# The triangular inverse of a gated delta-rule layer: T accumulated in its bank with one gathered weight tile per couple of batches, and the lists of a step reordered on four engines

## The reference

```
S = S * exp(g_t)                 # decay per key channel
err = k_t . S
S = S + k_t (x) beta_t (v_t - err)
o_t = q_t . S
```

## Time and profile before

| what | value |
|---|---|
| median of 3 runs | 5741.74 us (5737.70 to 5747.36) |
| the profiled execution | 5738.22 us, its span 5736.4 us |
| TensorE busy | 5429.4 us, 95% |
| VectorE busy | 4294.1 us, 75% |
| ScalarE busy | 3051.8 us, 53% |
| GpSimd busy | 1782.9 us, 31% |

### The profile page before, as it was taken

The page is one execution under the profiler, slowest core; times in us unless marked ns, Lnnn a source line. Parts: engine busy times, 40 slices in busy tenths (PEclk is TensorE's granted clock), DMA queues, the critical chain, the costliest instruction groups (busy, mean ns, idle before and its releaser), DMA issues. The chain is left out here.

```text
span 5736.4 us, 86704 instructions
## 1 busy us (share of the span) xinstructions
PE 5429.4 (95%) x28996; PEld 3752.5 (65%) x28996; DVE 4294.1 (75%) x8413; ACT 3051.8 (53%) x5964; POOL 1782.9 (31%) x1767
## 2 busy tenths in 40 slices
PE   5599999999999999999999999999999999799999
PEld 2377777777777777777777777777777777344444
DVE  7688888888888888888888888888888888121110
ACT  3466666666666666666666666666666665100110
POOL 2233333333333333333333333333333333000000
PEclk8799999999999999999999999999999999899999
DMA  2101111111111111111111111111111110331221
GB/s 77 47 29 38 30 38 30 38 30 36 30 36 30 35 30 38 30 38 30 38 30 38 30 37 31 32 37 30 38 30 38 30 30 19 107 112 52 72 75 50
DMA packets 192034, 235.65 MB, mean 41 GB/s; under 512 B 41577, under 2 KB 136425, under 8 KB 187505
## 3 DMA queue, kind: packets, MB, share of 16 engines
q1 hardware_dynamic: 111016, 188.22, 10.9%
q10 hardware_dynamic: 80584, 41.95, 2.5%
HBM read 183.75 MB, written 46.38 MB: 40 GB/s over the span
## 5 line engine op out<-in xcount | busy, mean ns | idle before, releaser
L720 PE MATMUL bank<-xT,weights 128*128 128x512 f32 x4096 | 2126.0, 606 | 33.2 <-PEq L155 33.2
L1465 POOL TENSOR_TENSOR KR<-KR,decay_u 128x256 f32<-128x256 f32 x768 | 691.2, 900 | 1536.4 <-PE bank L739 1536.4
L739 PEld LDWEIGHTS bank<-KQ,KR 128*128 128x128 f32 x7168 | 914.7, 191 | 266.0 <-issue 241.8
L739 PE MATMUL bank<-KQ,KR 128*128 128x128 f32 x7168 | 961.1, 276 | 16.3 <-DVE KQ L1040 15.4
L1040 DVE TENSOR_TENSOR KQ<-KQ,decay_u 128x512 f32<-128x512 f32 x896 | 746.2, 833 | 291.9 <-PE bank L739 291.0
L1025 DVE SCALAR_TENSOR_TENSOR conv<-pre,taps,conv 128x512 f32<-128x512 f32 x1152 | 936.8, 813 | 18.0 <-ACT conv L1254 8.3
L1055 DVE COPY_PREDICATED all_pairs<-level_mask,bank 128x512 f32<-128x512 int32 x896 | 792.8, 885 | 0.0
L720 PEld LDWEIGHTS bank<-xT,weights 128*128 128x128 f32 x4096 | 663.0, 192 | 185.9 <-issue 164.2
L762 PEld LDWEIGHTS bank<-T_inv,pairs 128*128 128x128 f32 x1536 | 270.9, 190 | 563.2 <-ACT T_inv L1319 323.0
L762 PE MATMUL bank<-T_inv,pairs 128*128 128x128 f32 x1536 | 495.2, 407 | 109.6 <-ACT T_inv L1319 109.4
L1319 ACT ACTIVATE T_inv<-bank 128x256 fp32r<-128x256 f32 x640 | 247.5, 387 | 454.0 <-PE bank L780 451.9
(11 more groups left out here) (190 smaller groups left out, 8963.4 us busy)
## 6 DMA issues: line engine op xcount, KB each, us to landing
decay_u<-decay_scratch SPq DMA_DIRECT2D x128, 510.0 KB
beta_u<-beta_scratch SPq DMA_DIRECT2D x128, 256.0 KB
y_in<-y_scratch SPq DMA_DIRECT2D x32, 1024.0 KB, 4.8
y_scratch<-y_rn ACTq DMA_DIRECT2D x112, 256.0 KB, 2.3
xt<-in_L_attn_hidden_states SPq DMA_DIRECT2D x8, 1024.0 KB, 5.3
x_in<-in_L_attn_hidden_states SPq DMA_DIRECT2D x28, 256.0 KB, 5.0
out<-o_out ACTq DMA_DIRECT2D x28, 256.0 KB, 2.0
w<-in_L_ffn_W SPq DMA_DIRECT2D x8, 704.0 KB, 4.8
```

Source lines behind the costliest of these rows:

```text
L720: last = nc.tensor.matmul(bank[w % 2][:], weights[par][:, w, k, :], xT[:, k, u % J * UC:(u % J + 1) * UC], start=k == 0, stop=k == KC - 1)
L739: last = nc.tensor.matmul(to[:, :, i], KR[:, cols(i)], halves(KQ[:, :, cols(i)], l, 1), start=True, stop=True)
L1465: nc.gpsimd.tensor_tensor(firsts, firsts, second.to_broadcast([P, 2, UC >> (l + 2), 1 << l]), ALU.mult).then_inc(keys_scaled.sem, 1)
```

## The change

X is kept in another order: its tile now has the turned batches first (2, 3, 0, 1; in_x), and so have the first pairs. T is no longer computed afresh from X. Bank 5 keeps T over the levels and each level adds to it. For this the product's weights are XX, a tile of 256 columns: for each couple the second sides of the natural batch's X and the first sides of the turned one's, side by side, gathered by three GpSimd copies (gather_x). The moving operand is Z without the identity, copied from its bank by ScalarE (keep_z). Z now lies in the upper half of bank 2. The first T comes from X by two matmuls of 256 columns, with a permutation that swaps neighbours as weights and neighbouring columns swapped in the moving operand (first_t); ScalarE takes it, and VectorE's first_inverse is gone. T and X of a level are separate entries of TensorE's list, and all four lists are reordered. ZI waits for keep_z, except at level 6.

```diff
@@ setup (GpSimd)
-            nc.gpsimd.tensor_copy(ident_r[:], ident[:])
+            nc.gpsimd.tensor_copy(swap_r[:].rearrange("p (m two) -> p m two", two=2)[:, :, ::-1],
+                                  ident[:].rearrange("p (m two) -> p m two", two=2))
@@ TensorE
-                for i in range(B):
-                    last = nc.tensor.matmul(bank[5][:, cols(i)], pairs_first[:, cols(i)], ident_r[:], start=True, stop=True)
+                for turned in range(2):
+                    to = slice(turned * (UC // 2), (turned + 1) * (UC // 2))
+                    at = in_x(turned * COUPLES) * P
+                    swapped = X[m % 2][:, at:at + UC // 2].rearrange("p (n two) -> p n two", two=2)[:, :, ::-1]
+                    last = nc.tensor.matmul(bank[5][:, to], swap_r[:], swapped, start=turned == 0, stop=turned == 1,
+                                            skip_group_check=True)
...
+            def inverse_t(l):
+                wait(pe, z_kept, b, l)
+                wait(pe, xx_ready, b, l)
+                for r in range(COUPLES):
+                    last = nc.tensor.matmul(firsts_in_place(bank[5], l, r), XX[:, cols(r)], Z[:, cols(r)],
+                                            start=False, stop=True, skip_group_check=True)
+                last.then_inc(t_done.sem, 1)
...
-                if l < LEVELS - 1:
-                    for i in range(B):
-                        last = nc.tensor.matmul(bank[5][:, half_cols(i)], X[b % 2][:, cols(i)],
-                                                halves(ZI[:, cols(couple(i))], l, i // COUPLES), start=True, stop=True)
-                    last.then_inc(t_done.sem, 1)
@@ VectorE
-                nc.vector.tensor_tensor(T_inv[:], bank[5][:], ident_each[:], ALU.add).then_inc(t1_ready.sem, 1)
...
-                wait(dve, z_done, b, l)
+                if l < LEVELS - 1:
+                    wait(dve, z_kept, b, l)
+                else:
+                    wait(dve, z_done, b, l)
@@ ScalarE
+            def keep_z(l):
+                wait(act, z_done, b, l)
+                nc.scalar.activation(Z[:], bank[2][:, UC // 2:UC], ACT.Copy).then_inc(z_kept.sem, 1)
...
+                nc.scalar.activation(all_first_sides(T_inv, l + 1), all_first_sides(bank[5], l + 1),
+                                     ACT.Copy).then_inc(t_ready.sem, 1)
@@ GpSimd
+        def gather_x(u, l, before):
+            if l >= 2:
+                wait_apart(pool, x_ready.sem, x_ready.at(u, l - 1), pool_waits_passed)
+                wait_apart(pool, t_done.sem, t_done.at(u, l), pool_waits_passed)
...
+            natural, turned = X[u % 2][:, UC // 2:], X[u % 2][:, 0:UC // 2]
+            nc.gpsimd.tensor_copy(halves(XX[:], l, 1), halves(natural, l, 1).bitcast(F32))
+            for i in range(COUPLES, B):
+                last = nc.gpsimd.tensor_copy(halves(XX[:, cols(couple(i))], l, 0),
+                                             halves(X[u % 2][:, cols(in_x(i))], l, 0).bitcast(F32))
+            last.then_inc(xx_ready.sem, 1)
```

More of the change, by code:

```diff
@@ L805, in apply_inverse @@
                 for i in range(B):
-                    last = nc.tensor.matmul(bank[7][:, cols(i)], X[u % 2][:, cols(i)], to[:, cols(i)], start=True, stop=True)
+                    last = nc.tensor.matmul(bank[7][:, cols(i)], X[u % 2][:, cols(in_x(i))], to[:, cols(i)], start=True, stop=True)
                 return last
@@ L918, in step @@
             level(0)
-            inverse_xt(1)
+            inverse_t(1)
             refine(c, 1)
+            inverse_x(1)
             project(2, (3,))
@@ L963, in step @@
             project(1, (2,))
[L964 removed]
+            first_t()
             project(1, (3,))
@@ L1395, in store_output @@
                                   by_batch(y_out[:])[:, :, 0:1], allow_slow_non_contiguous=True).then_inc(y_stored, 16)
+            keep_z(1)
             silu_v()
-            take_t(1)
+            take_t(b, 1)
             take_x(1)
+            keep_z(2)
+            take_projection(2)
+            take_t(b, 2)
+            take_x(2)
             store_output()
-            take_projection(2)
+            keep_z(3)
+            take_t(b, 3)
+            take_x(3)
+            keep_z(4)
             first_tap(2)
[L1403 to L1406, removed]
             silu_squares(0)
@@ L1409, in step @@
                 tail_squares()
+            take_x(4)
+            take_t(b, 4)
             square_output()
+            keep_z(5)
             silu_gate()
-            take_t(4)
-            take_x(4)
             silu_squares(1)
-            take_t(5)
+            take_t(b, 5)
             take_x(5)
@@ L1430, in step @@
             keep_all_pairs()
+            take_t(m, 0)
             take_projection(1)
@@ L1489, in step @@
                 squares_left(s.a, 1)
+                for l in range(2, LEVELS - 1):
+                    gather_x(s.b, l, None)
                 return
[L1491 to L1496, removed]
+            scale_keys(s.m, 1 - s.odd, 0)
+            gather_x(s.b, 2, None)
+            scale_keys(s.m, 1 - s.odd, 1)
+            gather_x(s.b, 3, None)
+            scale_keys(s.m, 1 - s.odd, 2)
+            gather_x(s.b, 4, None)
+            scale_keys(s.m, 1 - s.odd, 3)
+            first_x(s.m, s.c)
+            gather_x(s.b, 5, None)
+            scale_keys(s.m, 1 - s.odd, 4)
+            squares_left(s.a, 0)
+            scale_keys(s.m, 1 - s.odd, 5)
+            squares_left(s.a, 1)
+            scale_keys(s.m, 1 - s.odd, 6)
+            gather_x(s.m, 1, s.b)
         walk(pool, step)
```

163 lines of the change are left out of this document (92 added, 71 removed).

## The result

The changed kernel takes 5584.61 us (median of 4 runs, 5584.41 to 5589.27) where the kernel before takes 5743.07 beside it: ratio 0.9726, 95% interval 0.9710 to 0.9743. That is 158 us gained; 5540 was forecast, some 200 us. The direction and the range held; one term of the sum, the new waits, was off by half a microsecond a step.

What follows compares the result with a forecast made beforehand. TensorE was taken as the bound, VectorE close behind. Per step, 1.20 us less work and 0.37 less idle (0.97 old, 0.60 new) make 1.57, over 128 steps 201 us: 5540 us, own range 5495 to 5590, overall range 5450 to 5660.

Steps and rivals of the forecast that it cites:

- the new waits: TensorE's new small waits on ScalarE's copies, GpSimd's gathers and VectorE, put at 0.60 us a step.
- T's matmuls: TensorE, levels 1 to 5: twenty matmuls of 64 columns become ten of 128, removing 1.05 us a step.
- First T: TensorE: four matmuls of 128 columns become two of 256, between 0.11 us lost and 0.22 gained; 0.15 gained was taken.
- The split of T from X: Two visits of TensorE add no matmul; five more changes of kind cost 0 to 0.25 us, taken as 0.0.
- The old wait: TensorE's idle before Z, 0.82 us a step, ended by ScalarE's T copy; at Z(5) it goes as the silu moves.
- ScalarE's chain Z, copy, T: From Z's start through ScalarE's copy to T: 0.92 us, fitting TensorE's 1.08 us with 0.15 to spare.
- 0.8 hides with 0.3 to spare: GpSimd's gather of 0.8 us between X of one level and T of the next makes TensorE wait for nothing.
- Point 6: VectorE: 31.7 us of work in a step of about 34.6, late once or twice around levels 4 and 5.
- Rival 2: VectorE takes over as gathers hold it up: step 35 to 35.7 us, time 5600 to 5685; chance 0.20.
- rival 3: Slower: gathers on GpSimd delay T(2) to T(5); 1.9 us each gives 5870, 2.4 us gives 6130; chance 0.07.
- Rival 4: No effect: a wait at the step's end, from chain sums to level 0, sets the period; 5740; chance 0.03.
- Rival 1: Waits go wholly and TensorE's work shrinks by the upper bounds: at most 293 us, 5449; chance 0.14.

Runs made afterwards that it cites:

- experiment 4: The changed kernel with each T matmul of 128 columns issued as two of 64, same result: 5714.23 us, ratio 0.9952.
- Experiment 5: The kernel before with only ScalarE's square_output() and silu_gate() moved behind take_t(4) and take_x(4): 5650.77 us, ratio 0.9836.
- experiment 3: The changed kernel with each GpSimd gather cut to one copy of 2 columns, so T is computed from wrong weights: 5563.23 us, ratio 0.9685.
- experiment 1: The changed kernel with take_delta() put ahead of take_projection(0) in ScalarE's list: 5501.08 us, ratio 0.9583.
- experiment 2: The changed kernel with VectorE's tap convolve(1, (1,)) moved from ahead of ZI(4) to behind keep_pairs(3): 5631.18 us, ratio 0.9805.
- experiment 7: The changed kernel with take_delta() ahead of take_projection(0) and VectorE's gated_output() behind the two taps: 5464.24 us, ratio 0.9509.

## Why the prediction was right or wrong

- T's matmuls: 1.05 was taken, 0.95 measured by start to start (5 x 0.19), 1.01 by experiment 4. Right.
- First T: 0.15 taken, 0.16 measured (0.80 to 0.64). Right in the difference, by luck in part: the two prices that it came from were 0.44 and 0.22 to 0.55, and both groups take more from start to start. They start about 0.45 into the projection ahead, which takes 0.90 before a level; with it they take 1.25 and 1.10.
- The split of T from X costs nothing that can be seen: T's pairs take 0.25, X's 0.22 to 0.30 and 0.41 behind a projection at level 6, Z's 0.26 to 0.61 depending on what stands ahead, as before.
- The old wait: it went, as said, through the gate's place. It was worth more than its idle column, which is what the sum took. Experiment 5 gained 0.75 a step from it, of which 0.49 was idle time. That explains why busy time fell by 1.42 when 1.20 of work was forecast: 1.11 to 1.17 of work (T's matmuls and the first T as measured) and about 0.26 that the old wait had hidden in it. (Z(6) and the new waits hide some too, which this leaves aside.)
- ScalarE's chain Z, copy, T (0.92 of 1.08 us): it held. No wait for Z's copy appears before T. At level 3 it ran from 2586.75 (Z) to 2587.68 (end of the copy), 0.93. T(4) is taken only 0.50 us before Z(5) starts (2595.01 and 2595.51), not 1; that was still enough.
- New waits: this is the term of the sum that was wrong. It stood at 0.60, "new small waits (points 4 to 6)"; they are 1.13. Two make up 1.07 of it. 0.40 is T(4), where "0.8 hides with 0.3 to spare" is wrong for one gather in four, the one beside two taps: it took 1.60 (2591.04 to 2592.64), where level 3's took 0.65. (Level 1's took 1.61 in that step, where nothing waits; all gathers are 5.3 us a step, not 4.0.) And 0.67 is a wait that no point named: halo, projection copy, delta, refine. Point 6 expected VectorE to be late "around levels 4 and 5" and then looked only at what TensorE takes from it directly. What passed through ScalarE's list was missed. 0.53 x 128 = 68 us more idle, less the 0.22 x 128 = 28 us by which busy time fell further than forecast, is 40 of the 45 us between 5540 and 5585. So the time came out nearer than its terms: two errors, one of each sign, took part of each other away. 5585 is just inside the forecast's own range, 5495 to 5590.
- VectorE's work: 31.7 forecast, 32.5 measured. What experiment 3 took of the gathers, three quarters of their time, is 0.2 to 0.3 of it, not the 1.0 that was charged to them. The rest is in KQ, the taps and the halo copies; the groups answer to the earlier trace rows:

```profile
L1060 DVE SCALAR_TENSOR_TENSOR conv<-pre,taps,conv 128x512 f32<-128x512 f32 x773 | 674.9, 882 | 3.4
L1075 DVE TENSOR_TENSOR KQ<-KQ,decay_u 128x512 f32<-128x512 f32 x602 | 586.1, 974 | 34.7 <-PE bank L758 23.5
L1090 DVE COPY_PREDICATED all_pairs<-level_mask,bank 128x512 f32<-128x512 int32 x601 | 532.9, 887 | 0.0
```

  KQ went from 829 to 974 ns, the taps from 812 to 882, the 32-column halo copies from 703 to 1201, copy_predicated from 884 to 887. They now run beside GpSimd's squares and first_x (experiments 1 and 2 show a step of each); that the new order is the reason was not tried by itself.
- Rival 2 (VectorE takes over) is refuted by experiments 1 and 7, rival 3 by the gathers' time: at levels 2, 3 and 5 it was 0.64 to 0.65, and 1.60 at one level is not 1.64 at four. Rival 2's sum has a slip: 31.7 and 3.0 more are 34.7 us of work, not 33.7, and with the waits that it names its step is over 36 us, no gain at all; its range of 5600 to 5685 doesn't follow from its own terms. Rival 4 (the step's end sets the period) is refuted by the result and by experiment 4, where a longer T lengthens the step in full. Rival 1's size, 5449, was reached within 15 us by experiment 7, not by the change itself.

## What to carry to other kernels

When TensorE is busy for 97% of a step, the number of small matmuls is the price and can be read off start to start, and ten fewer were worth what the rows said. Price a wait the same way, from start to start with the group ahead of it: at Z(5) the idle column had 0.57 of 0.84 us, at T(4) 0.40 of 0.64. With lists in strict order, follow a late engine through the lists of the others: the two largest waits here each hung on one entry's place, and moving them gave 120 us on top of 158. Before an entry is moved, look at what it will run beside on the other engine and what stands behind it: a tap of 0.75 us took 1.36 beside first_x, ZI(6) came late, and the move cost 46 us.

## What the runs showed of the hardware that was not expected

- A copy of 32 columns on VectorE took 1.25 us beside a GpSimd square of two SBUF inputs, and ended 0.03 us after it (2604.89 and 2604.86). One of 16 columns with GpSimd idle took 0.17 us. In the stretch the copies of 32 columns take 1201 ns on average. So a short operation can be held up until the other engine's long one ends.
- The other way round two copies of 64 columns on GpSimd took 1.36 us beside two taps and 0.41 to 0.42 at three other levels.
- A GpSimd copy of 2 columns takes 270 ns (experiment 3) and one of 128 columns 290 ns: between these sizes the columns hardly count.
- TensorE's wait for an operand can stand for a third in its busy time: 0.27 of 0.84 us at Z(5), 0.24 of 0.64 at T(4).
